# A second layer in 32x32 array tiles instead of packed row sums, parts and a spread

## The reference

```python
def _L0_rec_ref(candidate_ad, goods, W1, b1, W2, b2):   # (2048,32), (2048,200,32)
    outer = jnp.einsum('bi,bnj->bnij', candidate_ad, goods).reshape(Bs, Ns, Ks * Ks)
    k_b = jnp.broadcast_to(candidate_ad[:, None, :], (Bs, Ns, Ks))
    h1 = jnp.concatenate((k_b, goods, outer), axis=-1)   # 32 + 32 + 1024 inputs
    act = jax.nn.sigmoid(h1 @ W1 + b1)                   # 36 hidden units
    weight = act @ W2 + b2                               # one weight for each good
    return jnp.sum(goods * weight, axis=1)               # (2048, 32)
```

## Time and profile before

| | us |
|---|---|
| median of 3 runs | 333.2 |
| profiled execution, its own time | 332.8 |
| span of the profiled execution | 330.7 |
| TensorE busy in the span (PE) | 307.9 (93%) |
| ScalarE busy (ACT) | 223.7 (68%) |
| VectorE busy (DVE) | 210.1 (64%) |
| GpSimd busy (POOL) | 183.1 (55%) |
| TensorE weight loads (PEld) | 153.4 (46%) |

### The profile page before, as it was taken

How to read it: one execution, slowest core, us unless ns; L and a number is a source line. 1 busy time by engine, 2 the same in 40 slices (tenths; PEclk the granted TensorE clock), 3 DMA queues, 4 the chain that set the end, 5 groups by cost and what they waited for, 6 DMA issues and landing times.

```text
span 330.7 us, 17422 instructions
## 1 busy us (share of the span) xinstructions
PE 307.9 (93%) x7480; PEld 153.4 (46%) x7480; DVE 210.1 (64%) x1114; ACT 223.7 (68%) x602; POOL 183.1 (55%) x261
## 2 busy tenths in 40 slices
PE   2992899999999999999999999999999999999993
PEld 1210355545555455545555555555555455554541
DVE  0999116656666666656666666666666566665676
ACT  0999667756667666666767766666777756676650
POOL 9300045566656566655565666566666666565663
PEclk9997579999999999999999999999999999999996
DMA  7970003645556656555666665565666646553000
GB/s 292 418 316 0 2 4 103 201 136 185 196 196 199 200 175 197 174 185 188 203 200 200 186 183 182 186 198 190 202 201 202 193 134 200 194 196 103 5 3 8
DMA packets 10588, 55.69 MB, mean 168 GB/s; under 512 B 1168, under 2 KB 1936, under 8 KB 10384
## 3 DMA queue, kind: packets, MB, share of 16 engines
q1 hardware_dynamic: 10080, 54.01, 49.6%
q10 hardware_dynamic: 432, 0.58, 0.5%
HBM read 54.32 MB, written 0.26 MB: 165 GB/s over the span
## 4 chain that ended last, share of the span: by engine, by line
PE 86%; ACT 9%; DMA 2%; issue 1%; DVE 1%; POOL 0%; POOLq 0%; ACTq 0%; DVEq 0%
PE z_ps L206 25%; PE w_ps L242 25%; PE s_ps L255 19%; PE x_ps L222 15%; ACT wm L290 5%; ACT wx L297 3%; DMA act<-w_outer 2%; ACT act L307 1%; DVE goods L349 1%; PE z_ps L176 1%; ACT L307 0%; ACT L290 0%; POOL mid L160 0%; POOLq L40 0%; DVE whole L342 0%
## 5 line engine op out<-in xcount | busy, mean ns | idle before, releaser
L349 DVE CUSTOM_DVE_ANT_0 goods<-s_ps,goods 128x200 f32<-128x200 f32 x512 | 161.5, 363 | 96.4 <-PE s_ps L255 88.5
L307 ACT ACTIVATE act<-z_ps,bias 128x200 f32<-128x200 f32 x512 | 169.7, 442 | 40.6 <-PE z_ps L206 40.6
L156 POOL TENSOR_SCALAR top<-whole,consts 128x200 bf16<-128x200 f32 x64 | 50.1, 784 | 124.9 <-DVE whole L342 124.9
L206 PE MATMUL z_ps<-goods,wm 32*32 32x200 f32 x4096 | 89.3, 346 | 10.4 <-ACT wx L297 7.2
L255 PE MATMUL s_ps<-stack,pick_sb 128*128 128x200 bf16 x512 | 78.4, 255 | 3.0 <-DVE out_stage L349 1.3
L206 PEld LDWEIGHTS z_ps<-goods,wm 32*32 32x32 f32 x4096 | 50.8, 104 | 43.6 <-issue 24.8
L222 PE MATMUL x_ps<-goods,wx 128*32 128x200 f32 x1024 | 69.4, 345 | 0.0
L255 PEld LDWEIGHTS s_ps<-stack,pick_sb 128*128 128x128 bf16 x512 | 32.8, 97 | 65.6 <-DVE out_stage L349 42.0
L312 ACT ACTIVATE actx<-x_ps,biasx 128x200 f32<-128x200 f32 x64 | 27.5, 429 | 45.6 <-PE x_ps L222 45.6
L242 PE MATMUL w_ps<-act,consts 128*32 128x200 f32 x1024 | 57.3, 342 | 0.0
L160 POOL TENSOR_SCALAR mid<-rest,consts 128x200 bf16<-128x200 f32 x64 | 50.1, 782 | 6.3
(11 more groups left out here) (26 smaller groups left out, 78.7 us busy)
## 6 DMA issues: line engine op xcount, KB each, us to landing
goods<-goods_t SPq DMA_DIRECT2D x64, 800.0 KB, 4.4
act<-cand_r SPq DMA_DIRECT2D x1, 1024.0 KB, 5.1
act<-cand_u SPq DMA_DIRECT2D x1, 256.0 KB, 5.9
pick_sb<-pick ACTq DMA_DIRECT2D x1, 256.0 KB, 8.3
out_t<-out_stage SPq DMA_DIRECT2D x4, 64.0 KB, 4.3
consts<-small ACTq DMA_DIRECT2D x1, 164.5 KB, 6.1
act<-w_outer ACTq DMA_DIRECT2D x1, 144.0 KB, 5.4
```

The source lines that it names most:

```text
L156: nc.gpsimd.tensor_scalar(top[:, :], whole[:, q % 2, :], m1, None, ALU.mult).then_inc(part_step, 1)
L206: last = nc.tensor.matmul(z_ps[32 * c:32 * c + 32, r, N * s:N * s + N], wm[32 * r:32 * r + 32, PAIR_U * p + 4 * s + c, :], goods[32 * r:32 ...
L307: last = nc.scalar.activation(act[:, p % A_SLOTS, r, N * s:N * s + N], z_ps[:, r, N * s:N * s + N], ACT.Sigmoid, bias=bias[:, r, p, s:s + 1])
L349: last = nc.vector.tensor_tensor_reduce(goods[:, q % G_SLOTS, v, :], s_ps[f % 2][:, N * i:N * i + N], goods[:, q % G_SLOTS, v, :], 1.0, 0. ...
```

## The change

The second layer (`row_sums`, `keep`, the parts and `spread`) becomes one step, `weights(q)`. It has 32 matmuls in 32x32 tiles with 400 moving columns (both halves of the pair's units). Their stationary operand is W2 repeated on 32 columns, so the weight of a good appears at once on all 32 partitions of its user. The first 16 multiply the 32 main hidden units, the other 16 add the 4 extra units on a K of 16. `keep`, GpSimd's four steps, the bf16 data and their load (`pick`) go. VectorE's custom instruction becomes a `scalar_tensor_tensor` that adds b2, multiplies by the goods and sums. `products_x` writes 400 columns in place of 200, and ScalarE reads them in two sigmoids. The eight PSUM banks become one tensor, and a table (`bank_table`) says which bank each step of each pair uses. `act` has two slots in place of three. Each pair's weights follow one pair behind (in place of three).

```diff
-A_SLOTS = 3
-LAG = 3
+A_SLOTS = 2
+XW = 4 * HX
...
+    z, x, s = {}, {}, {-1: [4, 5, 6, 7]}
+    for p in range(PAIRS):
+        z[p] = [0, 1, 2, 3] if p == 0 else z[p - 1][1:] + [s[p - 2][0]]
+        x[p] = z[p][0]
+        s[p] = [s[p - 1][1], x[p], s[p - 1][2], s[p - 1][3]]
+    return z, x, s
...
-            nc.gpsimd.memset(wx[:, :, :, :], 0.0).then_inc(wx_zeroed, 1)
-            pool.wait_ge(consts_loaded, 16)
-            for q in range(PAIRS):
-                pool.wait_ge(w_kept, q + 1)
...
+            nc.gpsimd.memset(wx[:, :, :], 0.0).then_inc(wx_zeroed, 1)
...
             pe.wait_ge(wb_kept[1], KEPT_ALL)
-            pe.wait_ge(pick_loaded, 16)
+            pe.wait_ge(bias_kept, 2)
...
# products(p)
-                        if s == 0 and p >= 1:
-                            pe.wait_ge(act_done, 4 * (p - 1) + r + 1)
+                        if s == 0 and p >= 1 and r < 3:
+                            pe.wait_ge(act_done, 4 * (p - 1) + r + 2)
+                        if s == 0 and p >= 2 and r == 3:
+                            pe.wait_ge(pooled, 4 * (p - 2) + 1)
...
+            def products_x(p):
+                pe.wait_ge(act_done, 4 * p + 1)
+                for s in range(2):
+                    for c in range(4):
+                        u = PAIR_U * p + 4 * s + c
+                        left = wx[:, u:u + 2, :].rearrange("p b m -> p (b m)")
+                        last = nc.tensor.matmul(banks[32 * c:32 * c + 32, x_bank[p], N * s:N * s + N], left,
+                                                goods[:, p % G_SLOTS, 4 * s + c, :], start=True, stop=True)
+                last.then_inc(x_done, 1)
+
+            def weights(q):
+                pe.wait_ge(act_done, 4 * q + 4)
+                for c in range(4):
+                    if c == 1:
+                        pe.wait_ge(actx_done, q + 1)
+                    elif q >= 1:
+                        pe.wait_ge(pooled, 4 * (q - 1) + max(c, 1) + 1)
+                    for r in range(4):
+                        nc.tensor.matmul(banks[32 * r:32 * r + 32, s_bank[q][c], 0:2 * N],
+                                         w2m[32 * c:32 * c + 32, :], act[32 * c:32 * c + 32, q % A_SLOTS, r, :],
+                                         start=True, stop=False)
+                for c in range(4):
+                    for r in range(4):
+                        last = nc.tensor.matmul(banks[32 * r:32 * r + 32, s_bank[q][c], 0:2 * N],
+                                                w2x[32 * c:32 * c + XW, r, :],
+                                                actx[32 * c:32 * c + XW, q % A_SLOTS, :],
+                                                start=False, stop=True)
+                    last.then_inc(s_done, 1)
+
+            for p in range(PAIRS + 1):
                 if p < PAIRS:
                     products(p)
+                if p >= 1:
+                    weights(p - 1)
                 if p < PAIRS:
+                    products_x(p)
...
# scalar engine, at the end of a pair
-                nc.scalar.activation(actx[:, p % A_SLOTS, :], x_ps[:, 0:N], ACT.Sigmoid,
-                                     bias=biasx[:, p:p + 1]).then_inc(actx_done, 1)
+                for s in range(2):
+                    last = nc.scalar.activation(actx[:, p % A_SLOTS, N * s:N * s + N],
+                                                banks[:, x_bank[p], N * s:N * s + N], ACT.Sigmoid,
+                                                bias=biasx[:, s, p:p + 1])
+                last.then_inc(actx_done, 1)
...
# vector engine, the loop over pairs
+            for q in range(PAIRS):
+                for c in range(4):
+                    dve.wait_ge(s_done, 4 * q + c + 1)
+                    for s in range(2):
+                        v = 4 * s + c
+                        u = PAIR_U * q + v
+                        last = nc.vector.scalar_tensor_tensor(
+                            goods[:, q % G_SLOTS, v, :], banks[:, s_bank[q][c], N * s:N * s + N], b2,
+                            goods[:, q % G_SLOTS, v, :], ALU.add, ALU.mult, out_stage[:, u:u + 1])
+                    last.then_inc(pooled, 1)
```

More of the change, by code:

```diff
@@ L6 @@
 F32 = mybir.dt.float32
-BF16 = mybir.dt.bfloat16
 ALU = mybir.AluOpType
@@ L182, in _ @@
                 src = cand[0:K, :, :].rearrange("i r (p s c) -> i c r p s", s=2, c=4)
-                last = nc.tensor.matmul(x_ps[32 * c:32 * c + 32, :], w1c[0:K, :], src[:, c],
+                last = nc.tensor.matmul(banks[32 * c:32 * c + 32, BIAS_M, :], w1c[0:K, :], src[:, c],
                                         start=True, stop=True)
@@ L187, in _ @@
             pe.wait_ge(wb_kept[1], kept_main(T_MAIN - 1, 1))
[L188 to L192, removed]
+            for c in range(4):
+                src = candu[:, :].rearrange("i (p s c) -> i c s p", s=2, c=4)
+                last = nc.tensor.matmul(banks[32 * c:32 * c + 32, BIAS_X, 0:2 * PAIRS], w1x, src[:, c],
+                                        start=True, stop=True)
             last.then_inc(bias_made, 1)
@@ L211, in products @@
                             last.then_inc(z_done, 1)
[L213 to L219, removed]
-                for c in range(4):
[L221 to L254, removed]
-                    last = nc.tensor.matmul(s_ps[f % 2][:, N * i:N * i + N], pick_sb[:, v, :], stack[:, q % 2, :],
-                                            start=True, stop=True)
-                last.then_inc(s_done, 1)
@@ L261, in _ @@
+            for p in range(PAIRS + 1):
                 if p < PAIRS:
                     products(p)
-                for f in (0, 1):
-                    if q >= 0:
-                        spread(q, f)
-                if 1 <= p <= PAIRS:
-                    row_sums(p - 1, 0)
-                    row_sums(p - 1, 1)
-                if q >= 0:
-                    spread(q, 2)
-                if 1 <= p <= PAIRS:
-                    row_sums(p - 1, 2)
-                if p < PAIRS:
-                    products_x(p, 0)
@@ L275, in _ @@
-                if q >= 0:
-                    spread(q, 3)
-                if p < PAIRS:
-                    products_x(p, 1)
+                if p >= 1:
+                    weights(p - 1)
+                if p < PAIRS:
+                    products_x(p)
         @block.scalar
@@ L301, in _ @@
                 if p >= A_SLOTS:
-                    sc.wait_ge(w_done, p - A_SLOTS + 1)
+                    sc.wait_ge(s_done, 4 * (p - A_SLOTS + 1))
                 for r in range(4):
@@ L334, in _ @@
             dve.wait_ge(bias_made, 2)
-            nc.vector.tensor_scalar(biasx[:, :], w_ps[:, 0:PAIRS], b1x, None, ALU.add).then_inc(bias_kept, 1)
-            def keep(p):
-                dve.wait_ge(w_done, p + 1)
-                if p >= 2:
-                    dve.wait_ge(part_step, 4 * (p - 2) + 2)
-                nc.vector.tensor_scalar(whole[:, p % 2, :], w_ps[:, 0:N], b2, None, ALU.add).then_inc(w_kept, 1)
-            def pool_units(q, f):
-                dve.wait_ge(s_done, 4 * q + f + 1)
-                for i in range(2):
-                    v = 2 * f + i
-                    u = PAIR_U * q + v
-                    last = nc.vector.tensor_tensor_reduce(
-                        goods[:, q % G_SLOTS, v, :], s_ps[f % 2][:, N * i:N * i + N], goods[:, q % G_SLOTS, v, :],
-                        1.0, 0.0, ALU.mult, ALU.add, out_stage[:, u:u + 1])
-                last.then_inc(pooled, 1)
@@ L354, in _ @@
-            for p in range(PAIRS + LAG):
-                q = p - LAG
-                for f in range(3):
-                    if q >= 0:
-                        pool_units(q, f)
-                if 1 <= p <= PAIRS:
-                    keep(p - 1)
-                if q >= 0:
-                    pool_units(q, 3)
+            nc.vector.tensor_scalar(biasx[:, :, :].rearrange("p s q -> p (s q)"), banks[:, BIAS_X, 0:2 * PAIRS],
+                                    b1x, None, ALU.add).then_inc(bias_kept, 1)
```

102 lines of the change are left out of this document (31 added, 71 removed).

## The result

The changed kernel takes 364.8 us (median of 4 runs, 360.4 to 368.2); the kernel before took 333.2 us in the same comparison. The ratio is 1.085 (95% interval 1.079 to 1.091): slower, where I forecast 299 us and faster. Its runs differ by up to 8 us, each with another mean granted clock (0.91 to 0.96), and the ratio is that of the two with the higher clock, 360.4 and 362.2 us, while the profiled one, 367.4 us with a span of 365.4 us, has a clock of 0.91.

The account below looks back on a forecast made before the run. TensorE's own order was taken to bound the kernel, at 4.35 us a pair. Start 54.3, 59 pairs of 3.85, interruptions 5.0, end 10.5 and 2.1 around the span gave 71.9 + 59 x 3.85 = 299.1 us; range 280 to 325.

Parts of the forecast that it names:

- interruptions that stay: Middle 59 pairs of the loop: 5.0 us beyond the pairs' own time, interruptions of the order, kept unchanged in the sum.
- what TensorE saves is saved: Whole loop: time saved on TensorE shortens the kernel until a loop through ScalarE or VectorE becomes as long.
- the prediction's own signs of being wrong: `weights` over 2 us with nothing waited for, ScalarE never idle, or the granted clock at half level inside the loop.
- the start: Up to pair 4, mostly at half clock: pair 4 starts 1.0 us later, at 54.3 in place of 53.3.
- TensorE's loop: TensorE's blocks of one pair, `products`, `weights` and `products_x`: 3.69 us, between 3.39 and 4.41.
- VectorE's loop: `weights` waits for `pooled` of the pair before, then eight VectorE instructions: 3.85 us, the longest loop, setting the pair's time.
- c: Price of one `scalar_tensor_tensor` on VectorE, start to next start: 0.33 us taken, between 0.285 and 0.42.
- the formula: Length of VectorE's loop in a pair: 1.21 + 8c us.
- ScalarE's loop: `products` of the next pair waits for this pair's last sigmoid: 3.44 us a pair, ten sigmoids fitting in it.
- The end: From the last `products` to the final store: 10.5 us in place of 15.4.
- dear native instruction: Rival on VectorE: sum's read not hidden, 0.42 us an instruction, pair 4.57 us, kernel 341.5 us; 12 in 100.
- doubled extra of the tiles: Rival on TensorE: `weights` 2.2 to 2.47 us, its loop 4.14 to 4.41, kernel 316 to 332 us; 13 in 100.

Follow-up runs that it names:

- b_noload: Kernel before the change with goods loaded for the first 8 pairs alone (56 of 64 loads left out): 327.1 us, ratio 0.985.
- b_split: Kernel before the change with each pair's goods load cut into four pieces: 326.8 us, ratio 0.982.
- b_dummy16: Kernel before the change with 16 tiny matmuls of 4 columns added in each pair's `products`: 389.0 us, ratio 1.172.
- a_bf16: Changed kernel with activations and W2 in bf16, so `weights` takes 64 records in place of 128 a pair: 283.7 us.
- a_noload: Changed kernel with goods loaded for the first 8 pairs alone and used again for the other 56: 327.9 us, ratio 0.987.
- a_split: Changed kernel with each pair's goods load cut into four DMAs, issued one by one as VectorE finishes steps: 352.9 us, ratio 1.059.
- a_noload_ttr: Changed kernel with goods loaded for the first 8 pairs alone and VectorE's custom multiply and sum for the native instruction: 319.2 us, ratio 0.960.
- a_bf16_split: Changed kernel with bf16 activations and W2 and each goods load in four pieces: 289.8 us, ratio 0.868.

## Why the prediction was wrong

- **What bounds the kernel before: right, but one row was passed over.** TensorE's order sets the pace. The sum carried 5.0 us as interruptions that stay. They were the same stretches, and b_noload and b_split show that they go with the loads' bursts. Asking for their cause would have shown that the fetch of a block's 256 records has to be done while TensorE works through the block in front.
- **The step that failed: "what TensorE saves is saved" counts time alone.** The sum said that `weights` has four passes; it did not count that the pair goes from 224 to 288 matmul and weight-load records. With its time of 4.30 us that is 67 records a us in place of 51. This cost (5.08 - 4.30) x 59 = 46 us in the profiled execution where 5 were allowed, stretches and the half clock behind them together. No rival had it. That records added alone bring the stretches, b_dummy16 shows: 28 in place of 5. Of the prediction's own signs of being wrong, the half clock level inside the loop came true.
- **The terms close the sum.** 46 - 5 us for this step, 27 us for the longer undisturbed pair (below), 1.5 us at the end and -0.7 us at the start (pair 4 starts at 53.6, not 54.3) make 69 us; the profiled execution is 68.3 us above the forecast.
- **Both causes count.** Without loads the stretches fall from 39.2 to 12.2 us, without the extra records (a_bf16, whose shorter `weights` changes the pair's time too) to 17.5 us, without both to none. The mean number of records in a us does not rank the kernels by itself: b_dummy16 with 59 (288 in 4.89 us) has 28 stretches, a_bf16 with 64 has 13. What decides is when a packet sets out against how long the block in front lasts. At 67 records a us a block lasts 3.8 us, 2.2 us of it are needed from the packet's start on, and half of the packets set out more than 1.86 us into the block; without loads (a_noload) it is 1.16 us, and in b_dummy16, whose blocks last 4.3 us, 2.56 us. Why packets set out that late even without loads no run shows.
- **Of the 46 us, some 14 are the half clock.** This is an estimate from the pairs' times. Ten pairs hold all of the 44 us at that level; they take 68.1 us, 11.2 of it stretches, and ten undisturbed pairs would take 43.0. The other 32 us are stretches. a_split's loop spent 20 us at the half level and a_noload's none.
- **`products` 1.14 and `products_x` 0.82: right** (1.13 and 0.81).
- **`weights`: mis-sized.** 1.97 us where I took 1.75; it pays 0.64 us above its 1.33 us of columns, about what `products` pays and not double. TensorE's loop is 3.93 in place of 3.69.
- **VectorE's loop: right in kind, too short.** c was 0.346 us (I took 0.33), so the formula gives 3.98; the pairs that meet this loop take 3.93 and 4.41 in turn, 4.17 on average, since only every second one waits for VectorE. Why they take turns stays open; with the faster custom instruction (a_noload_ttr) it is mostly 3.87 and 3.97, TensorE's own loop. The undisturbed pair, 4.30 on average, was 0.45 us above the forecast 3.85: 59 x 0.45 = 27 us.
- **ScalarE's loop: right** within 0.07 us, seen in the bf16 kernels.
- **The end: right in kind.** The last `products` starts at 353.4 and the span ends 12.0 us later (10.5 worked out, 15.4 before); in it the last `weights` waits 0.64 us for VectorE, which I had left out.
- **The rivals.** The dear native instruction (c = 0.42) is false: the read is hidden. The doubled extra of the tiles is false. What made the kernel slower was on no list. With the mis-sized terms alone the time would have been about 71.9 + 59 x 4.30 = 326 us, as a_noload's 327.9 shows from its side.

## What to carry to other kernels

Count the records of an engine, not only their time: here TensorE's program was itself data that came by DMA, one block of 256 records ahead, and TensorE stood still wherever a block was used up (3.8 us at 67 records a us) before the next had been fetched (a late start of 1 to 3 us, then at least 2.15 us), the more so behind large loads. When a profile shows "issue" waits of about a microsecond at equal distances in records, try shorter loads (one changed loop: 6 us for the kernel before, 9 for the changed one, but a loss in the bf16 kernel, so measure it), then fewer records. In this case the change that added records lost 28 to 32 us although its undisturbed pairs were no longer than before, and the same change without them (a_bf16) gained.

## What the runs showed of the hardware that I had not expected

- TensorE's program arrives in packets of 16 KB, 256 records. In all 14 traces the packet of a block set out 1.1 us before TensorE took up the block in front at the earliest, and mostly behind it. From the start of such a packet to TensorE's going on it took 2.2 to 2.5 us in the stretches looked at (packets of 0.88 to 0.97 us). During goods loads packets started about when the load ended: 75.90, 81.25, 85.90 and 91.79 us for loads that ended at 75.9, 81.5, 86.1 and 92.1.
- A 32x32 fp32 matmul of 4 columns cost 0.53/16 = 0.033 us of TensorE's time in the stream of `products`.
- Among stretches of 1 to 2.4 us, with TensorE busy between them, the granted clock fell to its half level (1.2 GHz) five times in the profiled execution, for 6.8 to 10.2 us each. In a_split, with stretches of up to 1.6 us, it fell six times for 3.4 us each. With no stretch above 1.3 us (a_noload) it never fell between the fifth pair and the last, nor with 28 stretches of up to 1.8 us in b_dummy16. So the length of the longest stretch alone does not tell when it falls.
- Four pieces in place of one load made the latest packets of the program earlier in all three kernels (a_bf16_split 2.39 in place of 2.89 us into the block, one in ten later), but in the bf16 kernel most of them later (middle value 1.71 in place of 1.37 us). That this gives its 25 stretches in place of 13 is read from the traces; no run tests it by itself.
